# Batch 3's attention ahead of the tile tables, and three second norms moved from GpSimd to VectorE and ScalarE

## The reference

```python
x = x + xattn(layernorm(x), ctx, ctx, Wq, bq, Wk, bk, Wv, bv)   # softmax(q k^T) v
x = x + moe(layernorm(x), w1, w2, router_w)
# moe: probs = softmax(x @ router_w.T); the two largest are the weights (not renormalised)
#      h = x @ w1[e].T;  y = silu(h[:, :256]) * h[:, 256:];  out += weight * (y @ w2[e].T)
# layernorm: (x - mean) / sqrt(var + 1e-5), without gain or bias
```

## Time and profile before

| | |
|---|---|
| device time, median of 3 runs | 142.17 us (140.96 to 142.18) |
| profiled execution, device time | 141.41 us |
| its span | 139.7 us |
| mean granted TensorE clock | 0.837 |
| TensorE matmul busy | 93.4 us, 67% |
| VectorE busy | 87.5 us, 63% |
| ScalarE busy | 60.7 us, 43% |
| GpSimd busy | 84.8 us, 61% |

### The profile page before, as it was taken

One profiled execution on the slowest core, in us unless ns is written; L12 is line 12 of the kernel. 1 busy time (PEld: TensorE's weight loads), 2 busy tenths in 40 slices (PEclk: granted clock), 3 DMA queues, 4 the chain that ended last, 5 costly groups with the idle time before them and its releaser, 6 DMA issues. The chain is left out here.

```text
span 139.7 us, 2773 instructions
## 1 busy us (share of the span) xinstructions
PE 93.4 (67%) x552; PEld 75.1 (54%) x552; DVE 87.5 (63%) x365; ACT 60.7 (43%) x147; POOL 84.8 (61%) x111
## 2 busy tenths in 40 slices
PE   1599960961171841867999979999989999950000
PEld 1599950851060310645878858888768778840000
DVE  6566999989838990277465435475945455428722
ACT  4223781642310239245555535555455555512430
POOL 8336433887777867777877663665555556777200
PEclk9999997555555586599999999999999999998555
DMA  2899990101111134332453233433332110078352
GB/s 62 232 297 352 409 386 31 61 19 59 59 54 40 36 68 126 113 97 78 120 122 100 79 100 78 113 97 95 99 92 57 60 41 17 25 260 278 117 216 75
DMA packets 14569, 16.83 MB, mean 121 GB/s; under 512 B 2423, under 2 KB 11208, under 8 KB 14424
## 3 DMA queue, kind: packets, MB, share of 16 engines
q1 hardware_dynamic: 11992, 11.90, 28.1%
q0 software_dynamic: 2272, 4.22, 9.3%
q10 hardware_dynamic: 288, 0.52, 1.0%
HBM read 10.38 MB, written 6.71 MB: 122 GB/s over the span
## 5 line engine op out<-in xcount | busy, mean ns | idle before, releaser
L476 POOL DMA_INDIRECT y_tok<-ob,xt x39 | 38.0, 975 | 22.2 <-DVE ob L968 14.2
L468 POOL DMA_INDIRECT x_sorted<-xn,slots x32 | 31.8, 993 | 12.3 <-issue 8.4
L960 DVE TENSOR_TENSOR y<-bank,sg 128x256 f32<-128x256 f32 x39 | 16.4, 424 | 17.9 <-ACT sg L589 17.2
L589 ACT ACTIVATE sg<-bank 128x256 f32<-128x256 f32 x39 | 15.0, 384 | 27.6 <-PE bank L1153 27.6
L1171 PE MATMUL bank<-w,yT 128*128 x156 | 20.9, 277 | 1.3 <-DVE ob L968 0.7
L1150 PE MATMUL bank<-w,xhT 128*128 x39 | 17.8, 455 | 4.3 <-ACT xhT L582 3.9
L1171 PEld LDWEIGHTS bank<-w,yT 128*128 128x128 f32 x156 | 19.0, 192 | 1.8 <-issue 1.8
L1153 PE MATMUL bank<-w,xlT 128*128 x39 | 15.9, 407 | 0.0
L1151 PE MATMUL bank<-w,xhT 128*128 x39 | 15.9, 407 | 0.0
L968 DVE COPY ob<-bank 128x256 f32<-128x256 f32 (+1 forms) x20 | 8.4, 418 | 10.7 <-PE bank L1171 10.7
L596 ACT ACTIVATE yT<-bank 128x512 f32<-128x512 f32 (+1 forms) x20 | 11.7, 586 | 1.4 <-PE bank L1162 0.5
(11 more groups left out here) (154 smaller groups left out, 152.8 us busy)
## 6 DMA issues: line engine op xcount, KB each, us to landing
xt<-x_sorted SPq DMA_DIRECT2D x39, 64.5 KB, 1.9
w_raw<-w_cols SPq DMA_DIRECT2D x4, 512.0 KB, 8.4
w_raw<-y_tok SPq DMA_DIRECT2D x3, 512.0 KB, 5.4
x<-x_rows SPq DMA_DIRECT2D x4, 256.0 KB, 6.4
xT<-x_cols SPq DMA_DIRECT2D x4, 256.0 KB, 6.7
w<-w_cols SPq DMA_DIRECT2D x1, 1024.0 KB, 11.5
out<-res SPq DMA_DIRECT2D x3, 256.0 KB, 3.2
y_tok<-ob,xt POOLq DMA_INDIRECT x39, 2.3
```

Source lines behind the costliest of these rows:

```text
L468: nc.gpsimd.indirect_dma_start(out=x_sorted, out_offset=bass.IndirectOffsetOnAxis(ap=slots[:, b, i:i + 1], axis=0), in_=xn2[:, b * J + j, ...
L476: nc.gpsimd.indirect_dma_start(out=y_tok, out_offset=bass.IndirectOffsetOnAxis(ap=xt[:, q % NX, i, D:W].bitcast(u32), axis=0), in_=ob[:, q ...
L589: nc.scalar.activation(sg[:, k % NSG, :], h_ps[k % 2][:, 0:F], ACT.Silu).then_inc(s_sg, 1)
L960: nc.vector.tensor_tensor(y[:, k % NY, :], h_ps[k % 2][:, F:2 * F], sg[:, k % NSG, :], ALU.mult).then_inc(s_y, 1)
```

## The change

On TensorE batch 3's `transpose_attn` is issued before `transpose_tables(0)`. The second norms of batches 1 to 3 leave GpSimd: VectorE adds eps and takes the reciprocal (`invert`), ScalarE takes the square root (`root`), and VectorE does one Newton step for 1/sqrt (`refine`). GpSimd keeps batch 0's, and its scatters then follow one another. ScalarE gets a one-element `Exp` after the first root. VectorE's list is reordered: the biases of batches 2 and 3 come earlier, and `full_tiles(1)` comes last.

```diff
+            def invert(b):
+                r = slice(b * J, (b + 1) * J)
+                dve.wait_ge(s_mv2, J * (b + 1))
+                nc.vector.tensor_scalar(veps2[:, r], mv2[:, r, 1], EPS, None, ALU.add).then_inc(s_veps2, 1)
+                dve.wait_ge(s_veps2, b + 1)
+                nc.vector.reciprocal(inv[:, r], veps2[:, r]).then_inc(s_inv, 1)
+            def root(b):                                   # ScalarE
+                act.wait_ge(s_inv, b)
+                nc.scalar.activation(near[:, b * J:(b + 1) * J], inv[:, b * J:(b + 1) * J], ACT.Sqrt).then_inc(s_near, 1)
+            def refine(b):                                 # VectorE, each step waits for the one before
+                dve.wait_ge(s_near, b)
+                step0 = near * near ; step1 = step0 * veps2 ; step2 = 1.5 - 0.5 * step1 ; rstd2 = step2 * near
 GpSimd:
-            second_norm(0)
+            second_norm()
             scatter(0, 0)
-            second_norm(1)
             scatter(0, 1)
-            scatter(1, 0)
-            scatter(1, 1)
-            second_norm(2)
-            second_norm(3)
-            for b in range(2, B):
+            for b in range(1, B):
                 scatter(b, 0)
                 scatter(b, 1)
 ScalarE:
             round_w1(7)
+            root(1)
+            nc.scalar.activation(act_warm[:], ones[:, 0:1], ACT.Exp)
             normalise(1)
             move_xw(3)
             softmax_exp(3)
+            root(2)
             move_eT(3)
             normalise(2)
+            root(3)
             normalise(3)
             nc.scalar.activation(act_warm[:], ones[:, 0:1], ACT.Silu)
 VectorE:
             second_stats(1)
+            invert(1)
             select(1)
             split_w1(0)
             split_w1(1)
             place(1)
+            refine(1)
             norm_bias(1)
             attend(2)
             second_stats(2)
+            invert(2)
             select(2)
             scores(3)
             score_max(3)
             place(2)
             full_tiles(0)
             split_w1(2)
+            refine(2)
+            norm_bias(2)
+            split_w1(3)
             move_tables(0)
-            split_w1(3)
             attend(3)
             second_stats(3)
+            invert(3)
             select(3)
             split_w1(4)
             split_w1(5)
+            refine(3)
+            norm_bias(3)
             place(3)
             fill_rows()
-            norm_bias(2)
-            full_tiles(1)
             split_w1(6)
             split_w1(7)
-            norm_bias(3)
+            full_tiles(1)
             split_x(0)
             move_tables(1)
 TensorE:
             count(2)
+            transpose_attn(3)
             transpose_tables(0)
-            transpose_attn(3)
             weigh_values(3)
```

More of the change, by code:

```diff
@@ L164, in xattn_moe_kernel @@
         nbias2 = sb("nbias2", [P, N])
+        inv = sb("inv", [P, N])
+        near = sb("near", [P, N])
+        step = sb("step", [P, 3, N])
         xn2 = sb("xn2", [P, N, 2, W])
@@ L271, in xattn_moe_kernel @@
         s_eT_ps, s_eT, s_av, s_x2 = sem("s_eT_ps"), sem("s_eT"), sem("s_av"), sem("s_x2")
+        s_inv, s_near, s_step = sem("s_inv"), sem("s_near"), sem("s_step")
         s_st2, s_mv2, s_veps2, s_rstd2, s_nb2, s_xn_v, s_xn_a = (
@@ L449, in first_norm, with second_norm @@
                 nc.gpsimd.tensor_tensor(rstd[:, r], veps[:, r], half_neg[:], ALU.pow).then_inc(s_rstd, 1)
[L451 to L456, removed]
+            def second_norm():
+                pool.wait_ge(s_mv2, J)
+                nc.gpsimd.tensor_scalar(veps2[:, 0:J], mv2[:, 0:J, 1], EPS, None, ALU.add).then_inc(s_veps2, 1)
+                pool.wait_ge(s_veps2, 1)
+                nc.gpsimd.tensor_tensor(rstd2[:, 0:J], veps2[:, 0:J], half_neg[:], ALU.pow).then_inc(s_rstd2, 1)
             def scatter(b, c):
@@ L746, in second_stats @@
                     nc.vector.bn_aggr(mv2[:, n, :], st2[:, n, :]).then_inc(s_mv2, 1)
+            def invert(b):
[5 more added lines that the diff above has]
+            def refine(b):
+                r = slice(b * J, (b + 1) * J)
+                done = 3 * (b - 1)
+                dve.wait_ge(s_near, b)
+                nc.vector.tensor_tensor(step[:, 0, r], near[:, r], near[:, r], ALU.mult).then_inc(s_step, 1)
+                dve.wait_ge(s_step, done + 1)
+                nc.vector.tensor_tensor(step[:, 1, r], step[:, 0, r], veps2[:, r], ALU.mult).then_inc(s_step, 1)
+                dve.wait_ge(s_step, done + 2)
+                nc.vector.tensor_scalar(step[:, 2, r], step[:, 1, r], -0.5, 1.5, ALU.mult, ALU.add).then_inc(s_step, 1)
+                dve.wait_ge(s_step, done + 3)
+                nc.vector.tensor_tensor(rstd2[:, r], step[:, 2, r], near[:, r], ALU.mult).then_inc(s_rstd2, 1)
             def norm_bias(b):
```

## The result

Over 22 runs of each, the changed kernel took 140.28 us in the median (139.05 to 143.92) and the kernel before 141.53 (140.49 to 142.52). The ratio is 0.9925, 95% interval 0.9899 to 0.9951: 1.1 us faster, between 0.7 and 1.4. I had forecast 3.5. That 140.28 lies inside my range of 137.0 to 140.4 is luck: the range was so wide because it took in rivals 1 and 2, and neither came about. The gain is a third of the forecast.

The account below looks back on a forecast made before the run. TensorE, ScalarE and VectorE in turn pace the expert loop; its start (2.7) and pair 8's stall (0.9), less 0.1, give 3.5 off 141.41: 137.9 profiled, 138.7 as median, middle 138.3 us. Range 137.0 to 140.4.

Parts of the forecast that it names:

- Rival 1: ScalarE's table switch takes twice its 1.28 us row, attend(3) 1.3 later: gain 2.2, time 139.6; chance 0.12.
- Rival 2: SyncE's queue becomes the bound, not held by batch 2's scatters; pair 8 waits again: gain 1.8, time 140.0; chance 0.1.
- no wait at pair 8: In the expert loop, group 2's loads come 3.7 us earlier, so TensorE's stall of 0.90 us goes.
- rival 4: Each ScalarE table switch takes X for 1.28 us: gain gone at 3.6, time 143.8 at 4.3; chance 0.05.
- Loop start: First expert matmul at 53.75 for 56.45, 2.7 us earlier, with 0.6 for reading expert numbers after table 1's transposes.
- one slow pair "as before": At the expert loop's start TensorE's clock is low for one pair only: 3.92 us against 3.12 for the next.
- rival 3: TensorE's clock: three more pairs of the expert loop run slow, 2.4 us lost, time 140.7; chance 0.08.
- My 3.6: Summed gain in us: 2.7 at the expert loop's start plus 0.9 at pair 8, before 0.1 taken off for rounding.
- margin of 0.1: At pair 8, rows ready for transposing from 79.1 us and TensorE arriving at 79.2.

Follow-up runs that it names:

- e1: The changed kernel with TensorE reading the first two expert numbers ahead of table 1's transposes, not behind them: ratio 0.9737 to the kernel before.
- e2: The kernel before with one edit, batch 3's transposes ahead of table 0's on TensorE: ratio 0.9884 to the kernel before.
- h2: The kernel before with only batch 3's transposes put ahead of table 0's on TensorE, measured again: ratio 0.9981 to the kernel before.
- h4: e1 with 18 artificial matmuls for 10: ratio 0.9768 to the kernel before.

## Why the prediction was wrong

**Right, up to the tables.** `attend(3)` 41.25 (forecast 41.6); `normalise(3)` over at 49.4 (49.8); table 1's transposes at 51.79 (52.15); group 0's loads at 45.85 (45.8); group 2's at 75.30 (75.0); no wait at pair 8. Batch 2's rows were there in time: GpSimd's scatters of batches 1 and 2 went at an even pace. Rival 1 falls, and so does rival 4: the switch on the path costs 1.28 with 0.03 around it. By the Trainium skill's page ScalarE: Activation LUTs (What ACT_TABLE_LOAD costs) it would have been 2.66; this trace, with 1.28, doesn't agree, though the engine is wanted at once. The row from which I took the price said so already: I wrote that nobody wanted ScalarE's work there, but the rounding at 55.94, for which TensorE waited, stood directly behind it. Rival 2 falls by its condition, since both groups of loads came when forecast.

**Wrong: the step "Loop start".** I put the reads of the expert numbers at 0.6, by the mean of the issue gaps ahead of L1138. Those gaps are what is left of the reads beside running matmuls. With nothing beside them the way from table 1's transposes to the row transposes is 1.84, where I had 0.65; e1 shows it by removal, 0.32, so the reads alone take 1.5, near the row's longest, 1.3. That is 1.2 too little. The row transposes at the low clock took 0.25 longer, and VectorE had been 0.4 earlier than forecast. So the first expert matmul came at 54.86 for 53.75: 1.1 us.

**Wrong: one slow pair "as before".** In the changed kernel's trace two pairs and the start of a third ran slow, at 3.91 us (54.86 to 58.77) against 3.12. From the first expert matmul to pair 3's it took 11.90 us (54.86 to 66.76), and 11.12 before (56.45 to 67.57): 0.8 us. I had priced more slow pairs, as rival 3 with a chance of 0.08. What I took for a property of the kernel was read from one execution: e2 and h2, one kernel, had two and one. That the gap ahead of the loop brings it, for which e1 and h4 speak, is argued and not shown.

**How the sum closes in the trace shown.** My 3.6 would have given a span of 136.1; it was 137.3, so 1.2 us are missing. The start accounts for 1.1 and the slow pairs for 0.8, together 1.9. The rest of the loop gave 0.7 back: pairs 3 to 8 took 15.57 us for 15.85 (the wait of 0.90 left out), and from pair 8's first expert matmul to the end it was 54.97 for 55.38. I had no term for either.

**What an ordinary execution loses beyond it.** The traces shown differ by 2.26 us (141.41 and 139.15), the medians by 1.25. That further 1.0 us can all lie behind pair 8: the 54.97 us are the least of eight traces in ordinary conditions, the others have 55.4 to 56.7, and the changed kernel's first execution 56.1. There pairs 12 and 16 came 3.38 and 3.41 us behind the ones ahead of them, and 3.09 in the trace shown. Why is open, and so is whether the change has a part in it.

**The next bound.** Rival 2 named the right place for a wrong reason. With a margin of 0.1 in my own working I should have said that further gains at the loop's start are soon taken at pair 8 by SyncE's list; h4 and h2 show such waits, 0.95 and 0.43 us.

**A better version.** e1, the changed kernel with the reads ahead of the table, beats both: 0.974 to the kernel before, in h4's form 0.977. It gives about what I forecast for the change, 3.7 us, by an edit that the forecast didn't have.

## What to carry to other kernels

When a reorder puts a wait ahead of register reads, the reads come onto the path at their full length; take that from where they stand alone, not from gaps beside running work, and move them ahead of the wait. Before counting a gain at the start of a loop, work out the next floor in it (here a transfer queue's list at pair 8): beyond it an earlier start and a faster clock buy little. Don't take the number of slow pairs from one execution. And one ratio holds for one set of conditions: this change was 0.75% faster in one and 4.9% slower in another.

## What the runs showed of the hardware

The granted clock in the profile can disagree with the matmuls. In the first execution of the changed kernel these rows of TensorE stand in a stretch at 1.00:

```profile
21.64 2.16 PE L1150 MATMUL bank<-v,eT 77*128 77x137 f32 x8 [0.83 <-DVE v L699]
```

```profile
22.00:23.00 1.00, 1.00 (x6) 1.00 (x6) 0.00 (x0) 0.99 (x2) 0.00 (x0) 1.00 0.00 0
```

Eight of these took 2.16 us, as at 0.50 (2.17). In the second execution the same eight took 1.17 us:

```profile
19.06 1.17 PE L1150 MATMUL bank<-v,eT 77*128 77x137 f32 x8 [0.83 <-issue]
```

It has the disagreement too, only earlier. Its recorded clock is 1.00 from the start to 22 us, and of two like groups of matmuls in that time the first took 1.84 us and the second 1.02:

```profile
13.31 1.84 PE L1130 MATMUL bank<-m,xT 128*128 128x85 f32 x8
...
16.30 1.02 PE L1130 MATMUL bank<-m,xT 128*128 128x85 f32 x8
```

The first execution took 143.92 us, and its mean clock was recorded as 0.917, higher than in the ordinary ones (0.806 to 0.845). Durations of like matmuls are the safer reading of the clock.

Two expert numbers read from a table into TensorE's registers take 1.5 us with nothing beside them (1.84 less 0.32, changed kernel and e1; 1.84 to 1.88 and 0.31 to 0.32 over thirteen traces).
